# Whole-row unpacking into two row buffers, compares of two chunks at once, and products of x over two row blocks

## What is computed

```
def _L0_gnn_ref(X, adj, W, b):
    deg = jnp.clip(jnp.sum(adj, axis=1, keepdims=True) + 1.0, 1.0, None)
    h_neigh = (adj @ X + X) / deg
    z = jnp.concatenate([X, h_neigh], axis=1) @ W + b
    out = jax.nn.relu(z)
    norm = jnp.linalg.norm(out, axis=1, keepdims=True)
    return out / jnp.maximum(norm, L2_EPS)

def _L1_gnn_ref(features, adj, W):
    deg = jnp.sum(adj, axis=1, keepdims=True)
    neigh = adj @ features / (deg + 1.0)
    return jnp.concatenate([features, neigh], axis=-1) @ W.T
x = _layernorm(x + _L0_gnn_ref(x, adj, L0_gnn_W, L0_gnn_b), axis=-1)
x = _layernorm(x + _L1_gnn_ref(x, adj, L1_gnn_W), axis=-1)
```

## Time and profile before

| | us |
|---|---|
| median of 3 runs | 813.52 |
| lowest and highest run | 813.45 and 820.82 |
| the profiled execution | 812.8 |
| its span, first to last instruction | 811.0 |
| busy in it: PE, DVE, ACT, POOL | 679.3 (84%), 725.9 (90%), 617.1 (76%), 254.0 (31%) |
| adjacency data moved | 256 chunks of 1 MB, 9.3 from issue to landing (median) |

### The profile page before, as it was taken

How to read it: one execution, slowest core, us unless ns; L and a number is a source line. 1 busy time by engine, 2 the same in 40 slices (tenths; PEclk the granted TensorE clock), 3 DMA queues, 4 the chain that set the end, 5 groups by cost and what they waited for, 6 DMA issues and landing times.

```text
span 811.0 us, 28070 instructions
## 1 busy us (share of the span) xinstructions
PE 679.3 (84%) x11157; PEld 625.5 (77%) x11157; DVE 725.9 (90%) x2782; ACT 617.1 (76%) x844; POOL 254.0 (31%) x302
## 2 busy tenths in 40 slices
PE   1688768687878797989898989989898989899992
PEld 0578658576768686878787979979797989899992
DVE  3346999989999999999999999999999999988994
ACT  2666969898979798988888887959695978860027
POOL 2012644314142434342525152513233332310014
PEclk9995868798989999989999999999999999999997
DMA  9925999999999999999999999989999899910004
GB/s 302 375 106 196 392 390 385 420 420 419 420 419 413 419 406 420 405 420 403 420 392 419 389 420 369 404 335 412 353 400 394 344 411 356 418 64 2 2 15 94
DMA packets 46283, 274.59 MB, mean 339 GB/s; under 512 B 12804, under 2 KB 12868, under 8 KB 13380
## 3 DMA queue, kind: packets, MB, share of 16 engines
q1 hardware_dynamic: 45184, 270.55, 83.7%
q0 software_dynamic: 576, 2.10, 0.7%
q10 hardware_dynamic: 388, 0.10, 0.1%
HBM read 270.63 MB, written 2.10 MB: 336 GB/s over the span
## 4 chain that ended last, share of the span: by engine, by line
DVE 37%; PE 34%; issue 11%; ACT 7%; DMA 7%; POOL 4%; DVEq 0%; SPq 0%; ACTq 0%
PE s_ps L363 15%; DVE e L758 11%; DVE t_sb L765 8%; DMA a_in<-in_adj 7%; ACT junk L562 6%; PE u_ps L381 5%; PE p_ps L349 4%; POOL small L1107 3%; DVE u_sb L765 2%; DVE q_sb L831 2%; DVE z_sb L809 2%; DVE y_sb L825 2%; PE u_ps L440 1%; PE p_ps L440 1%; PE z_ps L401 1%
## 5 line engine op out<-in xcount | busy, mean ns | idle before, releaser
L562 ACT ACTIVATE junk<-a_in 128x2048 uint8<-128x2048 uint16 x256 | 489.8, 1922 | 2.2 <-DMA a_in<-in_adj 2.1
L363 PE MATMUL s_ps<-yg,t_sb 128*128 128x129 f16 x4096 | 390.3, 252 | 27.7 <-DVE t_sb L765 23.9
L363 PEld LDWEIGHTS s_ps<-yg,t_sb 128*128 128x128 fp8e4 x4096 | 314.6, 103 | 58.9 <-DVE t_sb L765 29.7
L758 DVE TENSOR_SCALAR e<-a_in 128x2048 fp8e4<-128x2048 f32 x256 | 306.8, 1218 | 7.7 <-DMA a_in<-in_adj 7.6
L1115 POOL COPY store<-pk 128x32 uint32<-128x32 uint32 (+1 forms) x250 | 171.6, 729 | 371.2 <-ACT pk L571 371.2
L349 PE MATMUL p_ps<-pow_bf,e 128*128 128x16 bf16 x4096 | 142.7, 170 | 72.2 <-DVE e L758 67.4
L349 PEld LDWEIGHTS p_ps<-pow_bf,e 128*128 128x128 fp8e4 x4096 | 129.2, 97 | 89.6 <-DVE e L758 84.6
L765 DVE TENSOR_SCALAR t_sb<-pk 128x128 uint32<-128x128 uint32 x1024 | 151.4, 218 | 2.9 <-ACT pk L571 2.2
L1107 POOL TENSOR_TENSOR small<-small,minus_half 128x4 f32<-128x4 f32 x32 | 88.5, 2765 | 131.3 <-DVE small L819 66.7
L571 ACT CAST pk<-p_ps 128x512 uint8<-128x512 f32 x128 | 74.8, 584 | 34.0 <-PE p_ps L349 33.8
L381 PE MATMUL u_ps<-yg,u_sb 128*128 128x128 f16 x1488 | 100.5, 219 | 0.0
(11 more groups left out here) (112 smaller groups left out, 481.2 us busy)
## 6 DMA issues: line engine op xcount, KB each, us to landing
a_in<-in_adj SPq DMA_DIRECT2D x256, 1024.0 KB, 9.3
x_sb<-in_x POOLq DMA_DIRECT2D x4, 512.0 KB, 15.9
out_h<-e SPq DMA_DIRECT2D x8, 256.0 KB, 2.6
w_sb<-in_L_gnn_W ACTq DMA_DIRECT2D x1, 32.0 KB
w_raw<-in_L_gnn_W ACTq DMA_DIRECT2D x1, 32.0 KB
wy_sb<-in_L_gnn_W ACTq DMA_DIRECT2D x2, 16.0 KB
b_sb<-in_L_gnn_b ACTq DMA_DIRECT2D x1, 0.2 KB
wy_sb<-in_L_gnn_b ACTq DMA_DIRECT2D x1, 0.2 KB
```

The lines of the kernel that those rows point to most:

```text
L363: last = nc.tensor.matmul(s_ps[:, n % 2, at:GW], t_sb[:, b, :], yg[:, b, at:GW], start=(b == 0), stop=False)
L562: nc.scalar.activation(junk[:, t % 2, :], halves[t % R], ACT.Copy, scale=1.0 / 128, accum_out=half_sum[:, n, c:c + 1]).then_inc(s_half, 1)
L758: nc.vector.tensor_scalar(e8[:, c, :], a_in[:, t % R, :], 1.0, None, ALU.is_equal, saturate=False).then_inc(s_e, 1)
```

## The change

Four things change together.

- `compare` takes two adjacent chunks, 4096 elements, by one instruction. Its two waits on data stand together, and `s_e` goes up by two behind it.
- `unpack` takes a whole row block: 8 instructions of 256 words instead of 16 of 128. `t_sb` has two row buffers. It stands behind the first compare of the next row block and ahead of the second, and waits for the cast of both halves of `pk`.
- The four quarters of a row's sum are issued one chunk later, so that the last one falls into the row block after the next. The catching up moves from chunks 1 and 2 to chunks 2 and 3.
- The 16 groups of x products are spread over row blocks 1 and 2, two to a chunk, and every other `take_xt` goes from ACT to DVE. The packing of row block 0 no longer waits for the weights.

`normalise` moves ahead of the first compare of the third row block behind the batch, `transpose_h` behind the pack of chunk 1 and `dense_h` behind the pack of chunk 2; `take_g` stands behind the cast of the first half. The copy of the degrees `dcol` moves from DVE to POOL.

```diff
+LATE = 5
...
-        t_sb = sb("t_sb", [P, NB, P], FP8)
+        t_sb = sb("t_sb", [P, 2, NB, P], FP8)
...
+        def batch_at(n, k):
+            if n == BR + 1 + k:
+                return 0
+            return n // BR - 1 if n % BR == k and n // BR > 1 else None
+        def quarters(n, c):
+            if n < 2 or n == 2 and c == 0:
+                return []
+            if n < LATE:
+                return [(n - 2, c - 1) if c else (n - 3, 3)]
...
+            return [(n - 1, c - 1) if c else (n - 2, 3)]
...
PE, one row block
+                    if c == 1 and batch_at(n, 3) is not None:
+                        transpose_h(batch_at(n, 3))
+                    if c == 2 and batch_at(n, 3) is not None:
+                        dense_h(batch_at(n, 3))
...
-                    if n:
-                        sum_quarter(n - 1, c)
...
-                    if n >= START[1] and c in (1, 2):
-                        catch_up(n, c - 1)
+                    for r, i in quarters(n, c):
+                        sum_quarter(r, i)
+                    if n >= START[1] and c >= 2:
+                        catch_up(n, c - 2)
...
ACT, one row block
+                for c in range(NC):
+                    sum_codes(n, c)
+                    if n in (1, 2):
+                        take_xs((n - 1) * NC + c)
+                    if c == 0 and n:
+                        take_packed(n - 1, 1)
+                    if c == 1:
+                        for r in taken(n):
+                            take_sums(r)
+                        if batch_at(n, 3) is not None:
+                            take_h(batch_at(n, 3))
+                    if c == 2:
+                        take_packed(n, 0)
+                        if batch_at(n, 3) is not None:
+                            take_g(batch_at(n, 3))
...
DVE
-                nc.vector.tensor_scalar(e8[:, c, :], a_in[:, t % R, :], 1.0, None, ALU.is_equal,
-                                        saturate=False).then_inc(s_e, 1)
+                for i in (t, t + 1):
+                    dve.wait_ge(s_in[i % R], 16 * (i // R + 1))
+                if t >= NC:
+                    dve.wait_ge(s_pps, t + 2 - NC)
+                nc.vector.tensor_scalar(e8[:, 2 * h:2 * h + 2, :], a_in[:, t % R:t % R + 2, :], 1.0, None,
+                                        ALU.is_equal, saturate=False).then_inc(s_e, 2)
...
+            def unpack(n):
+                dve.wait_ge(s_pk, n * 2 + 2)
+                if n >= 2:
+                    dve.wait_ge(s_sum, n - 1)
...
DVE, one row block
+                if batch_at(n, 3) is not None:
+                    normalise(batch_at(n, 3))
                 compare(n, 0)
+                if n in (1, 2):
+                    split_y((n - 1) * NC)
+                    split_y((n - 1) * NC + 1)
                 if n:
+                    unpack(n - 1)
                 if n > START[1]:
                     add_piece(n - 1)
+                if batch_at(n, 2) is not None:
+                    residual(batch_at(n, 2))
                 if n >= START[1]:
                     unpack_piece(n)
+                if batch_at(n, 1) is not None:
+                    layer1(batch_at(n, 1))
+                compare(n, 1)
+                if n in (1, 2):
+                    split_y((n - 1) * NC + 2)
+                    split_y((n - 1) * NC + 3)
...
+                if batch_at(n, 3) is not None:
+                    low_part(batch_at(n, 3))
+                    begin_acc(batch_at(n, 3))
```

More of the change, by code:

```diff
@@ L220, in gnn_kernel @@
         s_acc = sem("s_acc")
+        s_dcol = sem("s_dcol")
+        s_xtd = sem("s_xtd")
         s_v = sem("s_v")
@@ L253, in lows, with taken @@
             return low(row_seg(n))
+        def batch_at(n, k):
[7 more added lines that the diff above has]
+                return [(n - 2, c - 1) if c else (n - 3, 3)]
+            if n == LATE and c:
+                return [(n - 2, 2 * c - 2), (n - 2, 2 * c - 1)] if c < 3 else [(n - 1, i) for i in range(3)]
+            if n == LATE:
+                return [(n - 3, 3)]
+            return [(n - 1, c - 1) if c else (n - 2, 3)]
+        def taken(n):
+            if n < 3:
+                return []
+            return [n - 3] if n <= LATE else [n - 3, n - 2] if n == LATE + 1 else [n - 2]
         agg_flat = agg[:, :, :, :].rearrange("p a k f -> p (a k f)")
@@ L258, in gnn_kernel @@
         cat, cat_t = (agg_flat[:, i * BR * P:(i + 1) * BR * P].rearrange("p (k f) -> p k f", f=P) for i in range(2))
-        nsum = s_sb
-        degp1, rdeg2 = (hs_flat[:, i * NB:(i + 1) * NB] for i in range(2))
+        nsum = q_sb = s_sb
+        degp1, rdeg2, w0_sb = (hs_flat[:, i * NB:(i + 1) * NB] for i in range(3))
         g_small = agg_flat[:, 2 * BR * P:2 * BR * P + 8 * BR].rearrange("p (s k) -> p s k", k=BR)
@@ L493, in _ @@
             pe.wait_ge(s_w1, 1)
-            for n in range(NB):
-                e, k = n // BR - 1, n % BR
-                if e >= 0 and k == 3:
-                    dense_h(e)
+            for n in range(1, NB):
+                begins, last_q = n == START[seg(n)], (low(seg(n)) - 1) // CB
                 for c in range(NC):
                     pack_chunk(n, c)
-                    if n == 1:
-                        for g in range(c * NE // NC, (c + 1) * NE // NC):
+                    if n in (1, 2):
+                        for g in range(((n - 1) * NC + c) * 2, ((n - 1) * NC + c) * 2 + 2):
                             if g == 0:
@@ L607, in take_y, with take_xs @@
                 nc.scalar.copy(y_hi[:, g * BR:(g + 1) * BR, :], y_ps[g % 2][:, :, F:2 * F]).then_inc(s_yhi, 1)
-            def take_xs(c):
-                for g in range(c * NE // NC, (c + 1) * NE // NC):
+            def take_xs(part):
+                for g in (2 * part, 2 * part + 1):
                     if g == 0:
                         take_xt(0)
-                    if g + 1 < NE:
+                    if g % 2 and g + 1 < NE:
                         take_xt(g + 1)
@@ L713, in _, with take_xt, split_y @@
             link(nc.vector.memset(x_t[F:F + 1, :, :, :], 1.0))
-            dve.wait_ge(s_w, 96)
+            dve.wait_ge(s_w, 80)
             nc.vector.tensor_scalar(wy_sb[0:F, F:2 * F], wy_sb[0:F, F:2 * F], YS, None, ALU.mult).then_inc(s_wy, 1)
-            def split_y(c):
-                for g in range(c * NE // NC, (c + 1) * NE // NC):
+            def take_xt(g):
+                dve.wait_ge(s_xtps, g + 1)
+                if g >= 2:
+                    dve.wait_ge(s_yps, g - 1)
+                nc.vector.tensor_copy(x_t[0:F, g % 2, :, :], xt_ps[g % 2][0:F, :, :]).then_inc(s_xtd, 1)
+            def split_y(part):
+                for g in (2 * part, 2 * part + 1):
+                    if g % 2 == 0:
+                        take_xt(g + 1)
                     rows = slice(g * BR, (g + 1) * BR)
@@ L766, in unpack_planes @@
                 return ins
[L768 to L774 removed]
+            def unpack(n):
+                dve.wait_ge(s_pk, n * 2 + 2)
+                if n >= 2:
+                    dve.wait_ge(s_sum, n - 1)
+                dst = words(t_sb[:, n % 2, :, :])
                 unpack_planes(lambda g: dst[:, :, g * PKW:(g + 1) * PKW],
[L776 removed]
+                              pk_w[:, n % 2, :].rearrange("p (b w) -> p b w", w=PKW)).then_inc(s_t, 1)
             def unpack_piece(n):
@@ L1108, in root, with degrees @@
                                         ALU.pow).then_inc(s_root, 1)
+            def degrees(e):
+                pool.wait_ge(s_agg, (e + 1) * BR)
+                nc.gpsimd.tensor_copy(dcol[:, e * BR:(e + 1) * BR],
+                                      agg[:, e % 2, :, 2 * HP:GW].rearrange("p k o -> p (k o)")).then_inc(s_dcol, 1)
             def keep(n):
@@ L1137, in general_pool @@
                     g_root_step(1, e + (2 * NE + 1))
-            for n in range(NB):
-                e, k = n // BR - 1, n % BR
-                if e >= 0 and k == 2:
-                    root(1, e)
-                if n:
-                    keep(n - 1)
-                if e >= 0 and k == 1:
-                    root(0, e)
+            for n in range(1, NB):
+                if batch_at(n, 1) is not None:
+                    degrees(batch_at(n, 1))
+                keep(n - 1)
+                if batch_at(n, 1) is not None:
+                    root(0, batch_at(n, 1))
+                if batch_at(n, 2) is not None:
+                    root(1, batch_at(n, 2))
             keep(NB - 1)
+            degrees(NE - 1)
             root(0, NE - 1)
```

134 lines of the change are left out of this document (37 added, 97 removed).

## The result

| | before | after |
|---|---|---|
| median of the runs, us | 817.17 (813.45 to 822.21, 4 runs) | 932.25 (930.66 to 934.47, 4 runs) |
| ratio, 95% interval | | 1.1418 [1.1361, 1.1475] |
| profiled execution: span, us | 811.0 | 928.8 |
| granted clock of TensorE, mean | 0.933 | 0.903 |

The change costs 115 us. The forecast was 902 with a range of 846 to 940.

What follows compares the result with a forecast made beforehand. The prediction had DVE and DMA binding the loop together at first, DVE and PE at last. It summed 812.8 + 56 + 22 + 5 + 5 - 2 + 3 = 901.8, forecast 902 us, range 846 to 940.

Steps and rivals of the forecast that it cites:

- the ring: Loop over row blocks: unpack, second compare, packs and cast wait in a circle through DVE, PE, ACT; +56 us, case's chance 0.48.
- products of x: Start of the kernel: spreading the 16 groups makes PE wait for DVE; +5 us, from 5 better to 10 worse.
- row blocks 3 to 11: Early loop without catching up: turn under 10 us but for layer1 and residual, guards hidden in slack; -2 us.
- clock: Loop: quarters run slow after PE's 26 waits for the second compare; 33 us if all, two thirds taken, +22 us.
- POOL: Loop: normalise waits for the power, which takes longer beside DVE's compares; +5 us, 0 to 15.
- last row blocks and the end: Last four row blocks +5 us; behind the last compare one more quarter and pack, +3 us (2 to 5).
- What the change takes off DVE: Row-block loop: unpacking 1.7 us instead of 2.4, pair compare 2.28 us, degrees' copy moved; 0.8 us a row block less.
- the sum of DVE: DVE's part of a late turn: unpacking with add_piece's wait until 2.0, adding, piece and compare; 6.3 us.
- the ring's sums: Loop: predicted lengths of four row blocks, 42.3 us (12 to 19) up to 51.1 (44 to 51), then 49.8.
- the turn over ACT at k = 3: Late row blocks: take_g and two sums on ACT stand ahead of the cast; 12.6 us, later than PE's way (11.9).
- 5 for the last four: Part of the +56 us for the loop: 5 us for the last four row blocks.
- the signs that the prediction named: Loop: DVE waits 1 to 2.5 us for casts, under 80% busy; PE waits 130 or more; clock under 0.9; 340 to 390 GB/s.

Runs made afterwards that it cites:

- e2: Changed kernel with each pair of chunks compared by two instructions of 2048 elements instead of one: 859.23 us, 1.0528 to the kernel before.
- e10: e9 with each pair compare given back as two compares of 2048: 814.97 us, 0.9975 to the kernel before.
- e5: Changed kernel with layer1 issued on DVE behind the row's second compare instead of in front: 885.81 us, 1.0838 to the kernel before.
- e4: Changed kernel with the third quarter also between the packs of chunks 2 and 3 from row block 12 on: 1013.95 us, 1.2431 to the kernel before.
- e6: e1 with adding the last piece and unpacking the next moved behind the row's second compare on DVE: 845.41 us, 1.0344 to the kernel before.
- e1: Changed kernel with the pack of chunk 3 directly behind that of chunk 2 from row block 12 on: 924.97 us, 1.1342 to the kernel before.
- e3: Changed kernel with 44 (k = 1) or 36 (k = 2) filler matmuls ahead of the pack of chunk 2 from row block 12: 897.18 us, 1.0984 to before.
- e9: e6 with layer1 also behind the second compare, and compares one pair earlier in row blocks 1 and 2: 819.61 us, 1.0032 to the kernel before.

## Why the prediction was right

The forecast's case held: the ring closes and sets the time. Each step against what was measured; its sum for the profiled execution (901.8) was 29 us short of what that took (930.7), and the last column adds up to that. All four lines are short, none is over, and the time lies 8 us inside the upper end of the range. The mechanism was right; that the number stayed in the range owes something to luck.

| step | forecast | measured | short by |
|---|---|---|---|
| products of x | +5 | +9 | 4 |
| row blocks 3 to 11 (measured to 14) | -2 | +10 | 12 |
| loop from 14 to 62: ring, clock, POOL | +51, +22, +5 | +89 | 11 |
| last row blocks and the end | +5, +3 | +10 | 2 |

- *What the change takes off DVE.* Right. The compare of 4096 takes 2286 ns and the next starts 2.27 us after it (290.5 / 128); I had 2.28 and 2.2. Unpacking costs 112.0 / 512 = 0.219 us an instruction, 1.75 a row block (1.7). DVE's busy time fell by 34 us. The Trainium skill, "VectorE: DVE Perf Modes", Rules for kernel authors, asks to keep the count of chained DVE operations small, since the pipeline is drained behind each. A fixed cost is there in this case (two instructions of 128 words take 0.296 us, one of 256 takes 0.219), and the runs show that it is no reason by itself to join two instructions when another engine waits for the first half: e2 and e10 are faster with more instructions.
- *The ring.* Shown by e5 (a step taken off it: -46 us), e4 (a step put on it: +82) and e6 (the second cut as well: -80 against e1), each with the same work. The length of a turn, added up from rows of before, is right within 0.2 us late in the loop where the clock doesn't disturb it (the table of e5). What I didn't see as a ring: the way through the catching up, almost as long. The prediction has it as a wait of `add_piece` ("until 2.0" in the sum of DVE), so the forecast holds it, but it made my first experiment fail. Also, the section on the change says that before "a compare stood between any two" of unpacking, adding, piece and `layer1`; its own listing has unpacking and adding side by side.
- *The clock.* The step that was mis-sized: "I take two thirds, +22 us". 14 waits of 2.9 us or more (3.25 to 4.30) stand in the trace between 380 and 780 us. Four of them, in row blocks 28 to 35, are ahead of a quarter with half of its matmuls wide, which takes 1.51 us at full clock and took 2.56 to 2.75 there; of the ten ahead of a wide quarter nine were followed by 3.09 to 3.60 us instead of 1.95. So 13 of 14 were slow, not two thirds. In 6 of the 14 the catching up behind the quarter was slow as well (1.37 to 1.91 us instead of 1.05), which I had left out, and so were the waits of 1.8 to 2.1 us at k = 0, behind which three of five quarters between 378 and 584 us were slow. e3, which takes away only those at k = 1 and 2, puts their price at 33 to 35 us in all, 27 in this stretch; the forecast for all was 22.
- *POOL.* "Sum 5 us" was wrong in size. The power did get longer, 3463 ns in the mean instead of 2765; with two compares of 2048 it is 2416 (e2). But the long one is now the power behind `layer1`, 4.46 us beside two pair compares, for which nobody waits soon. Behind `residual` it takes 2.9 to 3.4 us in most batches and ends with the compare beside it. That it lasts as long as the compares agrees with the Trainium skill, "SBUF — State Buffer", Who interferes with whom (a DVE instruction of this kind keeps the port pair that it shares with GpSimd for its whole length). DVE waited for it 0.9 us in the whole run.
- *The loop's remainder.* 89 measured, 51 for the ring and 27.4 for the clock by e3 leave 10.6 us. Some 4 are a slip of the recorded sum: its own lengths of four row blocks, weighted by the row blocks between the marks, add up to 567 us from 14 to 62, not to 171 + 190 + 202 = 563. The rest, 6 to 7 us, stands between row blocks 28 and 44, as the kernel with the clock kept shows (us for four row blocks, from second compare to second compare):

  | row blocks | 12 to 19 | 20 to 27 | 28 to 35 | 36 to 43 | 44 to 51 | from 52 |
  |---|---|---|---|---|---|---|
  | the ring's sums | 42.3 | 43.4 | 46.2 | 48.9 | 51.1 | 49.8 |
  | e3_clock_kept | 42.9 | 44.0 | 48.0 | 50.2 | 50.9 | 49.3 |
  | after | 44.9 | 45.6 | 49.7 | 52.7 | 54.1 | 53.0 |

  In these row blocks e3's trace has four waits at k = 0 without fillers (371.52, 420.09, 467.85 and 518.07 us), and the quarter and the catching up behind them take 6.3 us more than at full clock. That is an estimate from their rows, and it fits the 6 to 7 us; that all of it lies on the ring is argued, not shown. At k = 0 DVE meets a wait that I hadn't counted, 2.1 us for `take_g` in each batch (33.4 us, L877 above), but it lies beside the way over ACT that I did count (12.6 forecast, 12.4 measured).
- *Two smaller slips.* The terms of the turn over ACT at k = 3 ("= 12.6") add up to 12.8, the two sums being 1.9 us each. And "5 for the last four" row blocks counts two of them twice, since only 62 and 63 lie behind the mark of 62.
- *Row blocks 3 to 11.* The step that failed: "their ring is under 10 us", hence -2, where it was +10. Here DVE had set the pace before, busy for 103.3 of 108.9 us. In the changed kernel it has less to do, 98.5 us, but waits for some 20: 6.5 for the sums that `quarters` puts off (released by L390), 5.4 for `take_g`, 3.0 for the cast. PE waits for pair compares up to 3.53 us at once and 36.0 in this stretch, where it waited 15.9 for single ones before. Its clock isn't the difference (0.81, before 0.83). e2 has 110.5 us from 3 to 14 instead of 118.9: with single compares 8.4 of the 10 us are gone.
- *Products of x.* "From 5 better (all fast) to 10 worse (all slow)": it was the slow end. The transposes answer to the earlier trace rows:

```profile
54.18 1.04 PE L415 MATMUL u_ps<-ident,x_sb 128*64 128x128 f32 x4
...
56.72 1.06 PE L415 MATMUL c_ps<-ident,x_sb 128*64 128x128 f32 x4
```

1.04 to 1.06 us instead of 0.60 for 15 of the 16 groups, from 31 to 83 us; the last, at 86.88, took 0.60. The bubbles that I named (some 18 us of compares and unpacking) are there, but smaller, as waits of PE of 5.07, 3.46 and 3.33 us, and e9 gives 10 to 11 us back by filling them.

Of the signs that the prediction named, most came out on its side: DVE's waits for the cast (54 of them, 110.7 us, 2.05 in the mean, though single ones take 0.4 to 4.7), its share (75%), PE's wait (191 against "130 or more"), row blocks 46 to 62 at 211.7. Two did not: the clock is 0.87 from 200 to 300 us but 0.90 to 0.94 behind that, where "under 0.9" was asked, and the transfers fall from 386 to 313 GB/s in the course of the loop, where 340 to 390 were.

## What to carry to other kernels

When a change joins two small steps into one large one, write down for each step whom it waits for and who waits for it, and follow the names until one comes back: a circle through several engines sets a period that no engine's busy share shows. Its length can be added up from rows of the kernel before. Then look for the second circle before cutting the first, and take off the circle every step that only stands in its way in an engine's order; that was worth more (46 us for one moved call) than the work that the change saved (34 us of DVE). And a wait of TensorE can cost more than itself: behind 13 of the 14 waits of 2.9 us or more late in the changed kernel's loop the next matmuls were slow, and in e2 so were those behind three waits of only 1.81 us (at 658.73, 707.41 and 754.78), so add the slow work to the price of the wait at once.

## What the runs showed of the hardware

- In the products of x the granted clock is 1.00 in every stretch of 10 us from 30 to 90 us of the changed kernel, and four transposes take 1.04 to 1.06 us. In the kernel before, they took 0.60 at a granted clock of 1.00 (53.73) and 1.06 at 0.50 (63.00 us, the line below). So TensorE can run at the lower pace while the clock's record says full speed. In the changed kernel PE had been idle for 7.1 us before this stage and paused again and again in it. What sets the pace there no run tells.

```profile
63.00 1.06 PE L392 MATMUL c_ps<-ident,x_sb 128*64 128x128 f32 x4
```

- The same 16 wide matmuls cost 1.95 us, or 3.09 to 3.60 behind most of PE's long waits, and 80 more matmuls in four row blocks (e3) make the kernel 35 us faster.
- A compare of 4096 elements costs DVE 2.27 us, two of 2048 cost 2 x 1.17 = 2.34 (299.6 / 256, e2): joining saves 0.07 us a pair, 9 us in the kernel.
- An instruction of 256 words takes 0.219 us, one of 128 words 0.148: 0.077 us of an unpacking instruction are fixed.
